# Two instruction orders in a gated convolution: the next tile's diagonals on ScalarE, the 24-unit layer on TensorE

## The reference, cut to what matters

```python
x = x * y[:, :, None, None] + x                  # y: relu of a 96 x 96 product of weighted cell sums
pooled = x.mean(axis=(2, 3))
t = relu(gamma * (pooled @ w1.T - running_mean) * rsqrt(running_var + EPS) + beta)   # 24 units
wt = (t @ w2.T + b2).reshape(b * 96, 1, 3, 3) * MASK    # left-up, up, right-up and left remain
out = conv(x, wt, padding=1, groups=b * 96) + bias
```

## Time and profile before

| What | us |
|---|---|
| median of three runs | 212.09 |
| lowest and highest of them | 209.39, 212.86 |
| the profiled execution's own time | 210.17 |
| its span in the trace | 208.3 |
| busy in the span: TensorE, VectorE, ScalarE, GpSimd | 184.4, 167.4, 148.2, 132.4 |

### The profile page before, as it was taken

How to read it: one execution, slowest core, us unless ns; L and a number is a source line. 1 busy time by engine, 2 the same in 40 slices (tenths; PEclk the granted TensorE clock), 3 DMA queues, 4 the chain that set the end, 5 groups by cost and what they waited for, 6 DMA issues and landing times.

```text
span 208.3 us, 4493 instructions
## 1 busy us (share of the span) xinstructions
PE 184.4 (89%) x1678; PEld 106.4 (51%) x1678; DVE 167.4 (80%) x265; ACT 148.2 (71%) x274; POOL 132.4 (64%) x126
## 2 busy tenths in 40 slices
PE   7899999799889988998989988998899989999930
PEld 3448665356445554645554544554456645666610
DVE  3328789997898789879897889868987999789960
ACT  2021017968997989888998899789979975687710
POOL 0333029999999989977997979796970980134000
PEclk9999999999999999999999999999999999999995
DMA  5999999999999999999999999999999877568897
GB/s 137 365 424 430 424 429 423 429 333 361 422 422 424 431 424 426 425 426 426 429 417 440 425 426 424 427 426 432 431 426 417 345 323 271 219 216 292 281 336 254
DMA packets 9366, 79.34 MB, mean 381 GB/s; under 512 B 1248, under 2 KB 1888, under 8 KB 3328
## 3 DMA queue, kind: packets, MB, share of 16 engines
q1 hardware_dynamic: 9184, 78.95, 93.0%
q10 hardware_dynamic: 160, 0.10, 0.2%
HBM read 40.51 MB, written 38.54 MB: 380 GB/s over the span
## 4 chain that ended last, share of the span: by engine, by line
PE 40%; ACT 22%; issue 18%; DVE 11%; DMA 2%; POOL 2%; SPq 1%; DVEq 1%; ACTq 0%; POOLq 0%
PE banks L871 15%; PE banks L880 11%; ACT banks L715 11%; ACT xout L738 6%; ACT diag L711 6%; DVE xout L637 3%; PE banks L862 3%; DMA xout<-x 2%; PE banks L841 2%; PE banks L812 2%; DVE banks L637 2%; DVE xout L647 2%; PE banks L843 2%; POOL halves L406 2%; DVE stats L519 2%
## 5 line engine op out<-in xcount | busy, mean ns | idle before, releaser
L871 PE MATMUL banks<-xin,diag 64*64 64x495 f32 x576 | 129.4, 583 | 11.1 <-ACT banks L715 11.1
L880 PE MATMUL banks<-xin,diag 64*64 64x385 f32 (+1 forms) x768 | 134.5, 491 | 0.0
L406 POOL TENSOR_TENSOR halves<-xin 128x1568 f32<-128x1568 f32 (+1 forms) x22 | 73.8, 3356 | 27.7 <-DMA xin<-x 19.3
L715 ACT ACTIVATE banks<-xin,wide_sb,coef 128x504 f32<-128x504 f32 x95 | 76.4, 827 | 5.1 <-DVE xout L647 4.1
L880 PEld LDWEIGHTS banks<-xin,diag 64*64 64x64 f32 x768 | 49.7, 132 | 30.0 <-issue 21.5
L637 DVE SCALAR_TENSOR_TENSOR banks<-xin,coef,banks 128x825 f32<-128x825 f32 x48 | 51.7, 1078 | 14.0 <-ACT banks L715 14.0
L647 DVE SCALAR_TENSOR_TENSOR xout<-xin,coef,banks 128x495 f32<-128x495 f32 x72 | 52.2, 725 | 4.5 <-PE banks L871 4.5
L871 PEld LDWEIGHTS banks<-xin,diag 64*64 64x64 f32 x576 | 38.6, 132 | 29.6 <-ACT diag L711 16.9
L738 ACT ACTIVATE xout<-banks,wide_sb 64x392 f32<-64x392 f32 x72 | 41.9, 582 | 9.5 <-PE banks L880 8.0
L411 POOL TENSOR_TENSOR halves<-halves 128x784 f32<-128x784 f32 x18 | 33.3, 1849 | 1.4
L637 DVE SCALAR_TENSOR_TENSOR xout<-xin,coef,banks 128x825 f32<-128x825 f32 x24 | 25.6, 1068 | 0.0
(11 more groups left out here) (80 smaller groups left out, 114.2 us busy)
## 6 DMA issues: line engine op xcount, KB each, us to landing
xin<-x SPq DMA_DIRECT2D x23, 1568.0 KB, 12.8
out<-xout SPq DMA_DIRECT2D x18, 1568.0 KB, 13.7
out<-xout SPq DMA_DIRECT2D x5, 1176.0 KB, 4.5
out<-xout SPq DMA_DIRECT2D x10, 196.0 KB, 5.1
xout<-x SPq DMA_DIRECT2D x3, 392.0 KB, 4.7
xin<-x SPq DMA_DIRECT2D x1, 1120.0 KB, 14.9
out<-xout SPq DMA_DIRECT2D x1, 924.0 KB, 4.2
wide_sb<-wide SPq DMA_DIRECT2D x1, 467.5 KB, 15.9
```

The costliest lines, as they stand in the source:

```text
L406: eng.tensor_tensor(halves[:, j % 2, first:end, :], cells[:, :, 0, :], cells[:, :, 1, :], ALU.add).then_inc(once_folded, 1)
L715: return sca.activation(acc, above_rows(k, first, end), ACT.Identity, bias=bias[:, k % PER:k % PER + 1], scale=weight(k, UP))
L871: ins = mm(to[own], diag[own, k % 2, which, :], grid(k)[own, irows, cols], start=False, stop=(which == RIGHT_UP), skip_group_check=True)
L880: ins = mm(to[other], diag[own, k % 2, which, :], grid(k)[own, irows, cols], start=(which == UP), stop=(which == LEFT), skip_group_check=True)
```

## The change

ScalarE's loop: the four diagonals of tile k+1 (where tile k+1 is not crossed) move from behind the end of tile k's s chunk 0 (and, at t = 1, from behind `hidden_relu`) to ahead of it. TensorE's loop: at t = 1, `hide` moves from behind the third add of s chunk 1 to ahead of s chunk 1's first. No instruction is added or removed, and the semaphores are the same.

```diff
--- before.py
+++ after.py
@@ -756,13 +756,13 @@
                 seed_b(k, 2)
                 if t == 1 and g + 1 < NGROUP:
                     lift_relu(g + 1)
+                if k + 1 < TILES and not crossed(k + 1):
+                    for which in (LEFT_UP, UP, RIGHT_UP, LEFT):
+                        diagonal(k + 1, which)
                 finish_s(k, 0)
                 if t == 1 and g + 1 < NGROUP:
                     hidden_relu(g + 1)
                 if k + 1 < TILES:
-                    if not crossed(k + 1):
-                        for which in (LEFT_UP, UP, RIGHT_UP, LEFT):
-                            diagonal(k + 1, which)
                     act.wait_ge(coef_done, (k + 1) // PER + 1)
                     seed_b(k + 1, 0)
                     seed_b(k + 1, 1)
@@ -934,12 +934,12 @@
                 begin_b(k, 1)
                 end_s(k, 0)
                 end_b(k, 1)
+                if t == 1 and ahead:
+                    hide(g + 1)
                 begin_s(k, 1)
                 add_s(k, 1, LEFT_UP)
                 begin_b(k, 2)
                 add_s(k, 1, RIGHT_UP)
-                if t == 1 and ahead:
-                    hide(g + 1)
                 end_b(k, 2)
                 end_s(k, 1)
                 if t == 1 and ahead:
```

## The result

The changed kernel takes 213.05 us, the median of four runs (211.46 to 213.71), against 210.88 for the kernel before beside it (four runs). The ratio is 1.0144 with an interval of 1.0099 to 1.019: slower by about 1.4%, which is under 2%. The forecast was 212.8 us, 1.7 us or 0.8% over its base, in a range of 209.6 to 215.3. Executions of one kernel scatter by 1 to 2%, the longer ones mostly at a lower granted clock, so every kernel is compared with the kernel before run beside it. The profiled execution after took 211.46 us with a span of 209.5; the one before took 210.17 with 208.3.

What follows compares the result with a forecast made beforehand. No engine is full; an order of waits bounds the kernel. Terms 0.37 - 0.36 + 0.37 + 1.30 = +1.7 us on a base of 211.1 give 212.8 us, range 209.6 to 215.3.

Steps and rivals of the forecast that it cites:

- The barrier and its price: TensorE at t = 1: `hide` waits for both streams; its new place idles s 1.27 us and delays `make_taps` 0.83.
- A group: -0.09 forecast: Each of four groups from tiles 4, 7, 10 and 13: +0.37 - 0.46 = -0.09 us, so -0.36.
- Tile 7 to 8: Step at t = 1: tile 8 starts behind the later `make_taps`, at 92.01 instead of 91.64, +0.37 us.
- the hop from VectorE's coefficients to ScalarE: At t = 2, from coefficients' end to ScalarE's diagonals: 0.13 us, taken from a seed's end to the product.
- Tile 8 to 9: Step at t = 2: diagonals wait for VectorE's coefficients, 6.64 us instead of 7.10, -0.46, bounds -0.59 and -0.26.
- The last group: +1.30 forecast: Tile 19: `hide` waits for its input, `make_taps` at 178.14 instead of 176.84; +1.30 us goes through to the end.
- The first group: +0.37 forecast: Tiles 1 to 3: `make_taps` 1.29 us later, 0.46 of it idle before: +0.83, then -0.46, so +0.37.
- the edits worth nothing at t = 0: ScalarE at t = 0: same instructions in another order without a wait, 0 us, bounded by 0.1 either side.
- the sixth: Tile 16 to 17: +0.37 us, nothing given back, since the diagonals are GpSimd's from there.
- That the barrier does not hold the s stream: Rival at `hide`: s products pass it, groups gain 0.92 us, 5.1 in all, to 206.0; chance 0.12.
- The late loads: In the faster rival: six transfers need 22.5 us a group, more than 21.98, so part of the gain may return.
- The wait for the coefficients: Rival, ScalarE at t = 2: coefficients later by 0.5 us or more in five groups, 215.3 and above; chance 0.09.

Runs made afterwards that it cites:

- The full-shaped product: Kernel before, plus one full-array product of zeros (128 x 128 weights, 4 columns) at `hide`'s new place: 220.35 us, groups of 23.44.
- The kernel with tile 0's old order: Changed kernel, but in tile 0 the diagonals of tile 1 stay behind the end of s chunk 0: 211.12 us, ratio 1.0019 to the kernel before.
- the two looks: Two sets of runs of the kernel before with diagonals ahead in every tile, `hide` in its old place: 206.57 us beside 210.62, then 207.29 beside 210.28.
- the better version: Kernel before with diagonals ahead, `hide` in its old place: from tile 1 on 206.86 us (ratio 0.9807), in all tiles 207.29 (0.9824).

## Why the prediction was right, point by point

**The barrier and its price held.** `make_taps` later by 0.83 us was forecast and 0.82 measured; `hide` at 88.32, as worked out from tile 7 of before, is 2.92 after that tile's `mix` (85.40 in TensorE's timeline), and 2.92 was measured. The s stream stood idle as drawn. In one point the profile misleads. The weight loads' timeline after, which answers to the earlier trace rows:

```profile
88.88 0.14 PEld L849 LDWEIGHTS banks<-total,wide_sb 96*32 96x32 f32 x2 [0.78 <-DVE total L554]
```

It names VectorE's `total`. VectorE's timeline has this ready long before:

```profile
88.28 0.15 DVE L554 SCALAR_TENSOR_TENSOR total<-lift,banks 96x4 f32<-96x4 f32 x1
...
95.78 0.20 DVE L571 TENSOR_REDUCE coef<-spread 128x12 f32<-128x48 f32 x1
```

It ended at 88.43, 0.45 before the load. The full-shaped product, without that input, went at the same time, and its load is put down to yet another engine:

```profile
115.23 0.30 PEld L939 LDWEIGHTS banks<-zeros 128*128 128x128 f32 x2 [0.78 <-ACT xout L738]
```

That eviction ended at 112.95 (111.76 + 1.19 on ScalarE), 2.28 us before the load. So in none of the three cases does the profile name the stream that was waited for: it gives "issue" in the earlier trace rows, and here an engine whose part had long been done.

**A group: -0.09 forecast, -0.16 to -0.18 measured.** The forecast is half of what was measured, by one term. Tile 7 to 8 came out (8.70 instead of 8.35; +0.35 where +0.37 stood). The term that was mis-sized is the hop from VectorE's coefficients to ScalarE: they end at 95.98, and the diagonals start at 96.02, so it is 0.04 and not the 0.13 that was borrowed from the hop from a seed to a product. All else on this path came as worked out: coefficients 3.44 after the tile's start (3.43 forecast), from diagonals to seeds 2.19 (2.18), from there to the product 0.90 (0.90). Tile 8 to 9 is so 6.57 and not 6.64.

**The last group: +1.30 forecast, +1.21 measured**, by the same 0.13 for a hop. TensorE's timeline after, beside the earlier trace rows:

```profile
175.53 0.23 PE L849 MATMUL banks<-total,wide_sb 96*32 96x4 f32 x2 [0.32 <-DVE total L554]
...
178.43 0.84 PE L855 MATMUL banks<-hidden,narrow_sb 32*96 32x4 f32 x8
```

`hide` waited for its input here, as forecast, and went 0.05 after it (175.33 + 0.15 = 175.48 on VectorE), where 0.13 was put. `make_taps` stands 6.21 behind `mix` (172.22) and 5.00 before. That it goes through is right for VectorE: its coefficients in tile 20 wait 0.33 us for TensorE, where it was 0.20, and VectorE's last instruction starts 1.22 later against tile 19's `mix`. It is not right for the end of the span, which comes only 0.82 later: from VectorE's end to the last store it takes 0.4 less.

```profile
182.19 0.21 DVE L566 TENSOR_TENSOR spread<-banks,wide_sb 128x48 f32<-128x48 f32 x1 [0.33 <-PE banks L862]
```

**The first group: +0.37 forecast, +1.41 measured.** This step failed. At the full clock it is +0.21 (22.19 against 21.98), with the hop again; the rest, 1.2, is the clock. Nothing in the prediction asked what tile 0's new order would do: it was put among the edits worth nothing at t = 0, but it makes TensorE wait longer ahead of `mix`.

**The sum.** From tile 1's `mix` to the end the profiled span grew by 1.89 us, and 1.7 was forecast. By parts: +1.41 in the first group, -0.68 in four, +0.34 in the sixth (forecast +0.37), +1.21 in the last, and 0.4 less in the last stores, which no step had. So the total is nearer than its parts, and that is luck: the clock added some 1.2 that was not foreseen, and groups, stores and the last tiles came out some 1.0 lower. Without the clock the parts sum to 0.7. (The span as a whole grew by 1.2 only, since tile 1's `mix` stood 0.69 earlier in this execution, 40.75 instead of 41.44.) The kernel with tile 0's old order, which the prediction would price the same, says it again: 211.12 us beside 210.62 is +0.5 us, with an interval of -0.6 to +1.4 that does not hold the 1.7. The direction and the barrier's price were right; that the measured 213.05 lies 0.25 us from 212.8 owes as much to the clock. One bound of the prediction does not come out of its numbers: the times shown lie 1.7 us either side of the base, which gives 210.1 to 215.8 with its own range, and not 210.3 to 214.9. The range that it used, 209.6 to 215.3, is set by the rivals as well.

**The rivals.** That the barrier does not hold the s stream is refuted by the idle s stream, and its price is confirmed from the other side: where `hide` does not disturb, five groups gain 1.0 each, where 0.92 was worked out. The kernel as a whole was to gain 5.1 us. Its profiled span did, 203.2 beside 208.3 at the same mean clock of 0.988, but the medians of the two looks gained 4.1 and 3.0. The late loads that were to take back a part of it do come:

```profile
POOL halves L406 <- DMA xin<-x: 28.2, 12, 11.5
```

That is the waits view with the diagonals alone (us in total, times, longest); it was 19.3 us in 4 waits before. But the group stays at 20.97, so GpSimd's late sums hold nobody up in the middle of the kernel. The sixth group, from tile 16, is where a part is taken back: from `mix` to `mix` it takes 21.00 us, where it was 20.50 before and 20.04 would be left of that with 0.46 gained in tile 17. VectorE's timeline and TensorE's show a late store and what follows from it:

```profile
161.71 0.73 DVE L647 SCALAR_TENSOR_TENSOR xout<-xin,coef,banks 128x495 f32<-128x495 f32 x1 [0.88 <-DMA out<-xout]
```

```profile
167.03 0.67 PE L841 MATMUL banks<-by_image,wide_sb 128*96 128x4 f32 x6 [1.05 <-DVE by_image L547]
```

VectorE waits 0.88 us for an output buffer, works without a gap from there to `by_image`, and `mix` waits for that. Both kernels of the better version have the same wait, 1.06 and 0.92 us. So with the diagonals ahead a store is what the sixth group waits for. The wait for the coefficients took its place as named and cost nothing more than worked out.

## What to carry to other kernels

Where two streams of small-shaped products share TensorE and a product that waits for both stands between them, count both streams up to it and behind it, take the longer one on each side, and put the product where the sum is least: here 3.44, 3.61 and 4.27 us for three places. Moving a chain's product earlier brings nothing when its consumer stands behind the same streams. A change of two moves is worth one run for each alone: here the diagonals alone gain 1.8% (1.2 to 2.3) and `hide` alone loses 1.8% (1.0 to 2.6), and the two together lose 1.0 to 1.4%.

## What the runs showed of the hardware

The granted clock falls to its lower level (0.50, 1.2 of 2.4 GHz) for some microseconds within kernels whose TensorE is busy for about 90% of the span, and not at the same place in each execution. The windows view of the second run with the diagonals alone, in tile 0's start:

```profile
32.00:34.00 2.00, 2.00 (x3) 0.37 (x2) 1.86 (x3) 2.00 (x6) 1.83 (x1) 0.50 0.98 414
```

Ahead of it TensorE had issued the small products of the first chain, with products of zeros between them and an idle time of 0.82 us before `hide`. The idle time there does not decide alone: it was 0.33 in the repeat of the changed kernel, where the clock fell too, and 0.49 in the kernel before, where it did not, nor with 0.92 in the kernel with the diagonals ahead from tile 1 on. The other falls stand behind the idle times of 1.39 us (tile 1) and of 1.08 and 1.09 us (tile 19), but the first run with the diagonals alone has 1.40 and 1.05 in these places and kept 1.00 behind both. This goes with most of the scatter between executions: of the kernel before, the eleven runs of the last comparison took 209.5 to 210.8 us at mean clocks of 0.982 to 0.990 and 212.1 to 212.5 at 0.969 to 0.977. It doesn't go with all of it, as one run of the changed kernel took 212.78 at 0.991. What decides whether an execution falls stays open.
